# Cross-attention: scores from 64-row matmuls on the two row halves instead of stacked 128-row matmuls

## What is computed

```python
a = layer_norm(ctx, gamma, beta)
Q, K, V = x @ Wq.T, a @ Wk.T, a @ Wv.T            # each split in 16 heads of 64
scores = einsum('bhtd,bhsd->bhts', Q, K) * 64 ** -0.5
attn = softmax(where(mask, scores, -inf))
out = einsum('bhts,bhsd->bhtd', attn, V)          # heads put side by side again
y = x + tanh(gate) * (out @ Wo.T)
```

## Time and profile before

| | |
|---|---|
| median of 3 runs | 2229.86 us (2225.69, 2229.86, 2232.09) |
| the profiled execution, from first to last instruction | 2234.5 us, 0.2% above the median; no other time of it is given |
| TensorE (PE) busy | 2181.8 us, 98% |
| VectorE (DVE) busy | 1581.9 us, 71% |
| ScalarE (ACT) busy | 1380.7 us, 62% |
| GpSimd (POOL) busy | 1105.4 us, 49% |
| granted TensorE clock, mean | 0.995 |
| data moved by DMA | 219.96 MB, of them 128 KB in each of 256 swaps of keys by the page's count |

### The profile page before, as it was taken

How to read it: one execution, slowest core, us unless ns; L and a number is a source line. 1 busy time by engine, 2 the same in 40 slices (tenths; PEclk the granted TensorE clock), 3 DMA queues, 4 the chain that set the end, 5 groups by cost and what they waited for, 6 DMA issues and landing times.

```text
span 2234.5 us, 37000 instructions
## 1 busy us (share of the span) xinstructions
PE 2181.8 (98%) x10752; PEld 1791.5 (80%) x10752; DVE 1581.9 (71%) x3040; ACT 1380.7 (62%) x2620; POOL 1105.4 (49%) x887
## 2 busy tenths in 40 slices
PE   6999999999899999999999999999999999999998
PEld 4888788888688878888788887888878888788886
DVE  6666776667766677666876768666687666866666
ACT  4565675656556567566675566655675655856654
POOL 5544564445444455444554445544455444744443
PEclk9999999999999999999999999999999999999999
DMA  4323233332232323333233422323313233132222
GB/s 152 95 94 122 66 113 114 94 104 85 94 113 86 113 71 114 106 104 103 75 113 95 131 90 70 114 90 127 95 65 133 84 113 113 47 132 77 73 84 76
DMA packets 70612, 219.96 MB, mean 98 GB/s; under 512 B 10048, under 2 KB 11072, under 8 KB 69696
## 3 DMA queue, kind: packets, MB, share of 16 engines
q1 hardware_dynamic: 70592, 219.72, 30.5%
HBM read 169.35 MB, written 16.78 MB: 83 GB/s over the span
## 4 chain that ended last, share of the span: by engine, by line
PE 91%; DVE 4%; ACT 2%; issue 2%; DMA 0%; POOL 0%; SPq 0%; ACTq 0%; DVEq 0%
PE pj L352 15%; PE pj L356 15%; PE pj L354 15%; PE so L278 11%; PE pt L295 9%; PE pv L305 5%; PE pv L306 5%; PE so L324 3%; PE pv L319 3%; PE pv L320 3%; PE pv L324 3%; PE so L319 3%; PE so L320 3%; PE pj L286 1%; DVE pt_lo L595 1%
## 5 line engine op out<-in xcount | busy, mean ns | idle before, releaser
L735 POOL TENSOR_TENSOR w_lo<-w_raw,w_hi 128x1024 fp32r<-128x1024 f32 x253 | 608.7, 2417 | 451.8 <-ACT w_hi L422 343.5
L730 POOL TENSOR_SCALAR prob<-prob,rinv 128x512 f32<-128x512 f32 x512 | 353.7, 706 | 598.1 <-DVE rinv L575 596.8
L595 DVE TENSOR_TENSOR pt_lo<-pt,pt_hi 128x512 fp32r<-128x512 f32 x512 | 353.8, 691 | 226.5 <-ACT pt_hi L460 220.3
L570 DVE CUSTOM_DVE_ANT_0 prob<-so,mask_add 128x512 f32<-128x512 f32 x512 | 351.5, 691 | 194.2 <-PE so L278 186.7
L439 ACT ACTIVATE prob<-prob,nmax 128x512 f32<-128x512 f32 x512 | 369.5, 722 | 142.5 <-DVE nmax L570 138.9
L352 PE MATMUL pj<-a_hi,w_hi 128*128 128x512 f32 x1024 | 417.2, 407 | 2.3 <-POOL w_lo L796 1.4
L354 PE MATMUL pj<-a_lo,w_hi 128*128 128x512 f32 x1024 | 416.8, 407 | 0.0
L460 ACT CAST pt_hi<-pt 128x512 fp32r<-128x512 f32 x512 | 300.4, 587 | 187.3 <-PE pt L295 186.6
L356 PE MATMUL pj<-a_hi,w_lo 128*128 128x512 f32 x1024 | 411.5, 402 | 0.0
L278 PE MATMUL so<-k_st,q_st 128*128 128x512 f32 x1024 | 325.4, 399 | 10.1 <-DVE nmax L570 8.0
L295 PEld LDWEIGHTS pt<-ident,prob 128*128 128x128 f32 x2048 | 255.2, 140 | 70.5 <-POOL prob L730 1.3
(11 more groups left out here) (74 smaller groups left out, 3455.2 us busy)
## 6 DMA issues: line engine op xcount, KB each, us to landing
w_raw<-in_wq SPq DMA_DIRECT2D x65, 512.0 KB, 3.2
w_raw<-in_wk SPq DMA_DIRECT2D x65, 512.0 KB, 3.2
w_raw<-in_wv SPq DMA_DIRECT2D x64, 512.0 KB, 3.4
k_st<-k_st SPq DMA_DIRECT2D x256, 128.0 KB, 2.3
w_raw<-in_wo SPq DMA_DIRECT2D x64, 512.0 KB, 3.4
cx<-in_ctx SPq DMA_DIRECT2D x32, 512.0 KB, 5.4
xy<-in_xT SPq DMA_DIRECT2D x32, 512.0 KB, 4.6
out_y<-xy SPq DMA_DIRECT2D x7, 2048.0 KB, 6.3
```

Of the source, the lines that this page charges most:

```text
L570: dve.tensor_tensor_reduce(prob[:, u], so[u % 2][:], mask_add[:], -SCALE, BIG, ALU.add, ALU.min, nmax[:, u:u + 1]).then_inc(so_read, 1)
L595: dve.tensor_tensor(pt_lo[:, u % 2], pt[u % 2][:], f32(pt_hi[:, u % 2]), ALU.subtract).then_inc(pl_done, 1)
L730: pool.tensor_scalar(prob[:, u], prob[:, u], rinv[:, u:u + 1], 1.0, ALU.mult, ALU.mult).then_inc(scale_done, 1)
L735: pool.tensor_tensor(w_lo[:, kind], w_raw[:, w_slot(kind)], f32(w_hi[:, kind]), ALU.subtract).then_inc(wlo_done, 1)
```

## The change

Queries and keys are held as plain high and low tiles (`q_hi`, `q_lo`, `k_hi`, `k_lo`), with the two heads on the two partition halves as the projection leaves them. A group of scores is now one block t for both heads: three products (high x high, low x high, high x low; the low x low product is gone), each as two matmuls over 64 rows, the first on partitions 0 to 63 into bank `so[0]`, the second on partitions 64 to 127 into bank `so[1]`. There are four groups where there were eight units; `prob` is ordered by 2 t + h. The group waits until both banks have been read. The fillers behind the groups are 4, 4, 4 and 18. ScalarE and VectorE split q once and k once over 128 partitions, q behind the last exponential (before: its first half behind the seventh, its second behind the second transposed block). The swap DMAs, their tile copies and their semaphore are gone; `turn_p` waits for 7 scaled units for the first head and 8 for the second.

```diff
-FILL_S = (0, 4, 4, 4, 4, 4, 5, 5)
+FILL_S = (4, 4, 4, 18)
...
-        q_st = sb("q_st", [P, 2, T], F32R)
-        k_st = sb("k_st", [P, 2, 2, T], F32R)
+        q_hi, q_lo = sb("q_hi", [P, T], F32R), sb("q_lo", [P, T], F32R)
+        k_hi, k_lo = sb("k_hi", [P, T], F32R), sb("k_lo", [P, T], F32R)
...
                 load_w(WK, (j + 2) % PAIRS if isinstance(j, int) else j + 2, k)
-                swap_k(k)
-
-            def swap_k(k):
-
-
-                sp.wait_ge(kl_done, k * 2 + 4)
-                for h, (src, dst) in enumerate(((lo_half, hi_half), (hi_half, lo_half))):
-                    for order in range(2):
-                        sp.dma_start(f32(k_st[dst, h, order]), f32(k_st[src, h, 1 - order])).then_inc(kx_done, 16)
...
-            swap_k(-1)
             batch(0, first=True)
...
-            def scores(k, u):
-                h, t = divmod(u, TB)
-                if u == 0:
-                    pe.wait_ge(ql_done, k * 2 + 2)
-                    pe.wait_ge(kx_done, k * 64 + 64)
-
-                pe.wait_ge(so_read, k * 16 + (u + 1 if u < 2 else u + 3))
-                for order in range(2):
-                    mm = pe.matmul(so[u % 2][:], q_st[:, h, t * P:(t + 1) * P], k_st[:, h, order],
-                                   start=order == 0, stop=order == 1)
-                mm.then_inc(s_done, 1)
+            def scores(k, t):
+
+
+                if t == 0:
+                    pe.wait_ge(ql_done, k + 1)
+                    pe.wait_ge(kl_done, k + 1)
+                pe.wait_ge(so_read, k * 16 + (2 if t == 0 else 2 * t + 4))
+                cols = slice(t * P, (t + 1) * P)
+                for n, (q, kk) in enumerate(((q_hi, k_hi), (q_lo, k_hi), (q_hi, k_lo))):
+                    for h, rows in enumerate((lo_half, hi_half)):
+                        mm = pe.matmul(so[h][:], q[rows, cols], kk[rows], start=n == 0, stop=n == 2)
+                        if n == 2:
+                            mm.then_inc(s_done, 1)
...
                 if s == 0:
-                    pe.wait_ge(scale_done, k * UNITS + TB * (h + 1))
+                    pe.wait_ge(scale_done, k * UNITS + (UNITS - 1 + h))
                 pe.wait_ge(pl_done, k * UNITS + (u + 1))
                 for t in range(TB):
-                    mm = pe.transpose(pt[u % 2][:, t * P:(t + 1) * P], prob[:, h * TB + t, s * P:(s + 1) * P],
+                    mm = pe.transpose(pt[u % 2][:, t * P:(t + 1) * P], prob[:, 2 * t + h, s * P:(s + 1) * P],
                                       ident[:])
...
-                for u in range(UNITS):
-                    scores(k, u)
-                    if u == 0:
+                for t in range(TB):
+                    scores(k, t)
+                    if t == 0:
                         turn_v(k)
-                    take(stream, FILL_S[u])
+                    take(stream, FILL_S[t])
...
+            def q_high(k):
+                act.wait_ge(q_done, k + 2)
+                act.copy(q_hi[:], pj[1][:]).then_inc(qh_done, 1)
+
+            def k_high(k):
+                act.wait_ge(k_done, k + 2)
+                act.copy(k_hi[:], pj[0][:]).then_inc(kh_done, 1)
...
-                    if u == 6 and not last:
-                        q_high(k, 0)
+                if not last:
+                    q_high(k)
                 for u in range(UNITS):
                     p_high(k, u)
-                    if u == 1 and not last:
-                        q_high(k, 1)
...
                     if u == UNITS - 1 and not last and kind != "prepare":
-                        for h in range(2):
-                            k_high(k, h)
+                        k_high(k)
...
+            def q_low(k):
+                dve.wait_ge(qh_done, k + 2)
+                dve.tensor_tensor(q_lo[:], pj[1][:], f32(q_hi[:]), ALU.subtract).then_inc(ql_done, 1)
+
+            def k_low(k):
+                dve.wait_ge(kh_done, k + 2)
+                dve.tensor_tensor(k_lo[:], pj[0][:], f32(k_hi[:]), ALU.subtract).then_inc(kl_done, 1)
...
+                inverse_sums(k, 3)
                 if not last:
-                    q_low(k, 0)
-                inverse_sums(k, 3)
+                    q_low(k)
                 for u in range(UNITS):
                     p_low(k, u)
-                    if u == 1 and not last:
-                        q_low(k, 1)
...
                 if not last and kind != "prepare":
-                    k_low(k, 0)
-                    k_low(k, 1)
+                    k_low(k)
...
-                    if kind == "prepare" and n < 2:
-                        k_low(k, n)
+                    if kind == "prepare" and n == 0:
+                        k_low(k)
```

More of the change, by code:

```diff
@@ L101, in xattn_kernel @@
         w_ld = [sem("w_ld0"), sem("w_ld1")]
-        y_st, kx_done = sem("y_st"), sem("kx_done")
+        y_st = sem("y_st")
         so_read = sem("so_read")
@@ L336, in projections @@
                         if w == WV:
-                            pe.wait_ge(ql_done, 2)
+                            pe.wait_ge(ql_done, 1)
                     elif w == WQ:
@@ L345, in projections @@
                         pe.wait_ge(wlo_done, k * 4 + 6)
-                        pe.wait_ge(ql_done, k * 2 + 4)
+                        pe.wait_ge(ql_done, k + 2)
                     for i in range(KT):
@@ L526, in body @@
                     a_float(b, 1)
-                    k_high(k, 0)
-                    k_high(k, 1)
+                    k_high(k)
                     a_float(b, 2)
@@ L551, in _ @@
             act.copy(w_hi[:, WV], w_raw[:, 0]).then_inc(whi_done, 1)
-            q_high(-1, 0)
-            q_high(-1, 1)
+            q_high(-1)
             act.wait_ge(w_ld[1], 32)
             act.copy(w_hi[:, WQ], w_raw[:, 1]).then_inc(whi_done, 1)
-            for h in range(2):
-                k_high(-1, h)
+            k_high(-1)
             act.wait_ge(w_ld[0], 48)
@@ L580, in v_low @@
                                   f32(v_st[:, :, 0:4:3]), ALU.subtract).then_inc(vl_done, 1)
-            def q_low(k, h):
-                dve.wait_ge(qh_done, k * 2 + (3 + h))
-                src, dst = (hi_half, lo_half) if h else (lo_half, hi_half)
-                dve.tensor_tensor(q_st[dst, h], pj[1][src], f32(q_st[src, h]), ALU.subtract).then_inc(ql_done, 1)
-            def k_low(k, h):
-                dve.wait_ge(kh_done, k * 2 + (3 + h))
-                half = hi_half if h else lo_half
-                dve.tensor_tensor(k_st[half, h, 1], pj[0][half], f32(k_st[half, h, 0]),
-                                  ALU.subtract).then_inc(kl_done, 1)
+            def q_low(k):
[4 more added lines that the diff above has]
+                dve.tensor_tensor(k_lo[:], pj[0][:], f32(k_hi[:]), ALU.subtract).then_inc(kl_done, 1)
             def p_low(k, u):
@@ L716, in _ @@
                 build_mask(-1, step)
-            q_low(-1, 0)
-            q_low(-1, 1)
-            for h in range(2):
-                k_low(-1, h)
+            q_low(-1)
+            k_low(-1)
             run_loops(dve, body)
```

## The result

The changed kernel takes 2360.37 us (median of 4, 2357.10 to 2361.42), the kernel before 2230.98 us in the same comparison (median of 4, 2225.69 to 2236.02): a ratio of 1.0571 with a 95% interval of 1.0528 to 1.0614, 129 us slower. The forecast was 2345 us, 115 us slower, in a range of 2315 to 2475. The profiled spans differ by 2355.3 - 2234.5 = 120.8 us.

The account below looks back on a forecast made before the run. TensorE, 98% busy, was taken to set the time alone. Plain 63, prepare 20, switch 18, last 4.6, start -1.4 and form changes 11 summed to 115 us over the 2229.9 median: 2345 us, range 2315 to 2475.

Parts of the forecast that it names:

- The overlap (part 1): Score matmuls on TensorE: a pair of 64-row matmuls costs one pitch, 0.227 us, gaining 0.91 us per iteration.
- Rival B: Score groups: the two halves don't overlap, a group takes 1.36 instead of 0.68 us; 2469 us; chance 0.16.
- The loop (part 2): Plain score phase: from one group's start to the next, through VectorE's two row maxima, 2.47 us, TensorE idling 0.77.
- The chain to the seventh scaled unit (part 2): End of plain score phase: GpSimd's scaling is ready at 12.06 us, just covered by fillers ending at 12.22.
- The change of form (part 5): TensorE going to 64-row matmuls and back: 0.11 us each at the exposed entry and exit, 11 us in all.
- A2: Exposed changes of form: the array empties each time, 0.27 instead of 0.11 us, 18 us more: 2363; chance 0.14.
- Prepare (part 3): Seven prepare iterations: VectorE's statistics between row maxima lengthen the loop to 3.21 us; 2.9 us each, 20 in all.
- Switch (part 3): Seven switch iterations: late VectorE and GpSimd subtractions put scaling near 17.8 against 15.23 us; 2.6 each, 18 in all.
- Last, start: Last iteration without fillers: 12.06 against 7.48 us, 4.6 more; at the start, key swap DMAs gone, 1.4 us off.
- rival C: TensorE's clock: stalls in each iteration bring half speed to groups and fillers, 214 us more: 2559; chance 0.05.
- D: Waits of the three later groups: VectorE keeps up and 0.91 us is kept, 58 us off, 2172; chance 0.03.
- E: Score groups cost almost nothing on TensorE, less than a pitch in all; near 2237 us; chance 0.02.

Follow-up runs that it names:

- the run with the order alone: Kernel before with its stacked 128-row matmuls, put in the changed kernel's order (both banks filled, one wait, later transposes and q splits): 2348.07 us, ratio 1.0549.
- The even fillers: Changed kernel with fillers 5, 6, 6 and 13 behind the groups in place of 4, 4, 4 and 18: 2363.56 us, ratio 1.0620.
- one group: Changed kernel with all four score blocks back to back in banks so, pv, pt, so, then V's transposes and the fillers: 2273.73 us, ratio 1.0194.
- the best packed order found: Changed kernel with four score blocks back to back, and other engines' extra prepare and switch work moved later: 2224.92 us, ratio to before 0.9977.

## Why the prediction was right

**The overlap (part 1)** was taken as one pitch for a pair; measured 0.23 us from pair to pair. Rival B is out. The Trainium skill, "TensorE: Matmul & The Clock Gate", Part 3, agrees on the overlap. The same section says that matmuls start and end strictly in program order; the run with the halves in blocks contradicts that for matmuls on different row halves, and here the measurement decides.

**The loop (part 2)** was forecast at 2.47 us; measured 2.59 once and 2.48 in the others. The first group's terms, 2.31 and 0.06, make 2.37 and not the 2.40 written, which moves nothing. What I left out of the start is small: the first group starts as slowly as the others (0.33 us to its second pair), so its results come 0.1 later and the first loop takes 2.47 where I had 2.40. In the second loop the row maximum starts 1.23 us behind its group (442.01 to 443.24 in VectorE's timeline) in place of 1.11; with the stacked matmuls this loop took 2.48. That extra 0.12 I can't place. The stalls came as forecast in place and cause, but the view has 0, 0.49 and 0.39 us of idle time in a plain iteration where I had 0.35, 0.77 and 0.77, and 76.8 us in all where I had some 120: 0.16 of each (0.389 - 0.227) is the last matmul still in flight, and 0.20 goes to a change of form that hides there. The run with the order alone (12.45 us, as computed) shows the loop by itself.

**The chain to the seventh scaled unit (part 2)** was forecast to end 0.16 us ahead of the fillers. The even fillers bear it out: with five fillers fewer behind the last group (1.14 us) the first transpose starts only 0.29 us sooner behind it (4.83 in place of 5.12) and waits 0.65 us for GpSimd.

**The change of form (part 5)** was undersized: 0.11 us taken, 0.20 measured (0.19 by two differences of kernels). The nearest row, a change from transposes, was not near enough; the bound of 0.27, a full emptying of the array with a slow restart, was not reached either. The Trainium skill, "TensorEngine Tiling (Array Packing)", Key Properties, has the array drain at a change of tiling mode; starts 0.32 to 0.33 us apart are nearer to a last matmul that must end (0.39) than to a pitch, so its direction is borne out. Of the rivals A2 (2363 us) is the nearest to the median, but that is partly luck: its price of 0.27 was too high, as 0.11 was too low. That changes at an idle TensorE hide was right. Exposed in a plain iteration are 0.10 us at the entry, 0.20 at the exit and 0.07 in the first loop: 0.37 us, 18 us in 49 of them, where I had 0.22 and 11. With the loop's 0.12 this is most of the gap in the plain iterations, 1.80 us each in place of 1.51 (88 us in place of 74).

**Prepare (part 3)**: 20 us forecast, 20 measured, the score phase 14.03 us where I had 14.3. The 0.5 us that I took off for small stalls had no row behind it; the phases grew by 3.1 us and the iterations by 2.8.

**Switch (part 3)** was wrong on both sides: 18 us forecast, 9 measured. I took 15.23 us as the phase of before from one iteration, and the starts of all seven show 11.4 in four of them and 15.2, 15.4 and 13.8 in three: the stall of 2.42 us at the start and the slow clock behind it are not the rule. And I let the changed kernel inherit that late VectorE (17.8 us) where every one of its switch phases takes 15.5. The trace of before shows what makes VectorE late. These are the same two subtractions in a switch iteration with the stall and in one without:

```profile
557.32 2.40 POOL L735 TENSOR_TENSOR w_lo<-w_raw,w_hi 128x1024 fp32r<-128x1024 f32 x1 [2.29 <-ACT w_hi L422]
557.42 2.84 DVE L615 TENSOR_TENSOR x_lo<-xy,x_hi 128x512 fp32r<-128x512 f32 x1
...
285.93 2.78 POOL L735 TENSOR_TENSOR w_lo<-w_raw,w_hi 128x1024 fp32r<-128x1024 f32 x1 [2.55 <-ACT w_hi L422]
285.78 0.68 DVE L615 TENSOR_TENSOR x_lo<-xy,x_hi 128x512 fp32r<-128x512 f32 x1
```

Where VectorE's subtraction starts 0.10 us behind GpSimd's it takes 2.84 us (2.84 or 2.85 in all three stalled iterations); where it starts 0.15 ahead, 0.68. In the traces of before and after, behind the first 60 us, a subtraction `x_lo` of VectorE starts 20 times 0.1 to 1.3 us inside a subtraction of GpSimd's, and each time it ends 0.55 us behind the end of that one: VectorE's waits until GpSimd's is done. (It started once 6 ns behind one, and took 0.68.) In the changed kernel the last `x_lo` ahead of a switch iteration's first row maximum starts 0.46 or 0.47 us ahead of GpSimd's and took 0.68 in all seven. So the small 9 us is partly luck of the profiled execution: against a before with 34.1 us in all seven switch iterations it would be 27. The profiled execution of before also had one switch iteration of 45.6 us, 11.5 more than the usual 34.1, part of it a mask conversion that took 6.6 us on VectorE where six of the other seven took 0.5 (the first, at the start, 1.5). Its span is 3.5 us over the median of before, and that of the changed kernel 5.1 us under its own, which is why spans give 121 us and medians 129.

**Last, start**: 4.6 and -1.4 forecast. The last score phase grew by 12.17 - 7.48 = 4.7, the last iteration by 5.3, and the start gained 1.5.

**The sum** was forecast at 115 us and came to 121 in spans and 129 in medians. The plain iterations' 14 us too little and the switch ones' 9 too much stand against each other, so that the total is nearer than its terms.

**The clock** (rival C) stayed at 1.00 in the phases shown, through idle times of 0.39 and 0.49 us in plain iterations (TensorE at 93% busy) and of up to 0.99 in prepare and switch ones. In the last iteration, where no fillers stand between groups (4.46 busy of 12.17, idle times of 0.92 and twice 1.51 us), it was 0.88 on average. **D and E** fell with the loop.

## What to carry to other kernels

Packing two short contractions side by side on the array works and costs one pitch for two, but each switch between packed and full matmuls costs 0.20 us here: it pays only if the packed ones stand together in long runs, with banks enough to hold them (the plain phase took 12.66 us with the groups apart in two banks, 11.60 in four, 10.69 in one run, 10.93 before). When two banks are filled together and read together, the filling and the reading engine alternate, and the loop is the sum of both; count it before counting matmuls. And look at the iterations with extra work by themselves: pairing the heads moved the wait at the first transpose from the fourth to the seventh scaled unit, and with one group the plain iterations gained 9 us while the 14 others lost 41. That the longer wait is the reason fits the idle time there, but no run changed it alone.

## What the runs showed that I had not expected

Matmuls on the two row halves don't keep the program's order between halves: written lower, lower, lower, upper, upper, upper, they ran two by two, with the same time (2360.71 against 2360.37 us). A change of form costs 0.20 us in either direction, half of it ahead of the first matmul of the new form and half behind it. And the kernel before, with stacked operands and four products in two full matmuls, is level with the best packed order found (2224.92 us, ratio 0.9948 to 1.0005), although that one has four slots fewer. A subtraction on VectorE that starts inside one of GpSimd's waits for its end: 2.84 us in place of 0.68 in the three switch iterations of before that have the stall of 2.42 us.
